# Attention and a routed expert layer on one core: gate data in the rows, gated copies, gathers that add

## The reference, cut to what matters

```python
    x = x + _L0_xcond_ref(_layernorm(x, axis=-1), ctx_2048, ctx_2048, itok_B_779_1933)
    x = x + _L0_ffn_ref(_layernorm(x, axis=-1), L0_ffn_gate_w, L0_ffn_w1, L0_ffn_w2, L0_ffn_w3)

    # attention
    s = SCALE * jnp.log(k_length.astype(jnp.float32))[:, None, None, None]
    attn = jax.nn.softmax(s * jnp.einsum('bhdq,bhdk->bhqk', qh, kh), axis=-1)
    out = jnp.einsum('bhqk,bhdk->bhdq', attn, vh)
    # experts
    probs = jax.nn.softmax(jnp.einsum('ti,ei->te', xt, gate_w), axis=-1)
    expert_weights, expert_indices = jax.lax.top_k(probs, 2)
    expert_weights = expert_weights / expert_weights.sum(axis=-1, keepdims=True)
    y[e] = (silu(xt @ w1[e].T) * (xt @ w3[e].T)) @ w2[e].T
    out = sum over the two chosen experts of expert_weights * y[expert]
```

## Time and profile before

| what | value |
|---|---|
| median of 3 runs | 1231.14 us (1230.88 to 1231.62) |
| the profiled execution | 1232.27 us, of which the span from first to last instruction is 1230.7 us |
| mean granted TensorE clock | 0.951 |
| busy, of the span | TensorE 1035.8 us (84%), VectorE 810.9 (66%), GpSimd 638.4 (52%), ScalarE 410.7 (33%) |

### The profile page before, as it was taken

How to read it: one execution, slowest core, us unless ns; L and a number is a source line. 1 busy time by engine, 2 the same in 40 slices (tenths; PEclk the granted TensorE clock), 3 DMA queues, 4 the chain that set the end, 5 groups by cost and what they waited for, 6 DMA issues and landing times.

```text
span 1230.7 us, 19877 instructions
## 1 busy us (share of the span) xinstructions
PE 1035.8 (84%) x5081; PEld 413.9 (34%) x5082; DVE 810.9 (66%) x953; ACT 410.7 (33%) x734; POOL 638.4 (52%) x578
## 2 busy tenths in 40 slices
PE   1799988999998998832999999999999999999910
PEld 0123322333333333211444444444444444444400
DVE  5877877888888887213853954938677395953354
ACT  3266666666666676721111111111100111011100
POOL 6454766676767762322841834807566182830055
PEclk9699999999999999975999999999999999999965
DMA  6465655565555552105875756647666575753387
GB/s 175 153 223 150 186 153 175 174 189 181 175 177 181 179 150 70 48 27 161 203 141 143 185 132 171 171 96 212 153 197 176 147 191 149 191 133 86 71 227 257
DMA packets 212839, 195.58 MB, mean 159 GB/s; under 512 B 137376, under 2 KB 176288, under 8 KB 207392
## 3 DMA queue, kind: packets, MB, share of 16 engines
q1 hardware_dynamic: 198624, 123.80, 38.5%
q0 software_dynamic: 14176, 71.31, 17.7%
HBM read 111.44 MB, written 52.95 MB: 134 GB/s over the span
## 4 chain that ended last, share of the span: by engine, by line
PE 49%; POOL 20%; DMA 11%; issue 10%; DVE 7%; POOLq 2%; ACT 1%; SPq 1%; DVEq 0%
PE rows L1072 23%; PE heads_out L1072 12%; POOL W L423 7%; PE heads_out L989 4%; PE scores L976 4%; DVE nm L717 3%; PE rows L962 3%; DMA rb<-recips_dram 3%; POOL W L422 3%; DMA recips_dram<-rden 2%; DMA U<-wpack_dram 2%; POOL us L500 1%; POOL us L497 1%; PE misc L1039 1%; POOL U L422 1%
## 5 line engine op out<-in xcount | busy, mean ns | idle before, releaser
L1072 PE MATMUL rows<-W,U 128*128 (+1 forms) x1776 | 391.9, 381 | 23.6 <-DMA U<-stage 19.5
L717 DVE TENSOR_REDUCE nm<-rows 128x2 f32<-128x1024 f32 x256 | 304.2, 1216 | 61.2 <-PE rows L962 53.1
L598 ACT ACTIVATE W<-scores 128x512 f32<-128x512 f32 x512 | 283.9, 596 | 153.0 <-PE scores L976 151.7
L1072 PEld LDWEIGHTS rows<-W,U 128*128 128x128 bf16 x1776 | 174.3, 98 | 236.0 <-issue 30.4
L663 ACT ACTIVATE U<-rows 128x512 f32<-128x512 f32 x78 | 46.4, 597 | 520.3 <-PE rows L1072 511.5
L962 PE MATMUL rows<-W,U 96*128 96x512 bf16 x512 | 151.6, 400 | 71.0 <-DVE nm L717 43.6
L1072 PE MATMUL heads_out<-W,U 128*128 x888 | 199.4, 381 | 13.3 <-issue 10.6
L423 POOL TENSOR_TENSOR W<-U,W 128x2048 bf16<-128x2048 f32 x42 | 172.6, 4110 | 7.7 <-POOL W L422 7.7
L900 DVE TENSOR_TENSOR U<-rows,U 128x512 f32<-128x512 f32 x78 | 53.6, 687 | 183.6 <-ACT U L663 183.5
L976 PE MATMUL scores<-U,W 128*128 128x512 bf16 x512 | 168.1, 386 | 5.6 <-ACT W L598 4.7
L907 DVE TENSOR_TENSOR U<-U 128x512 bf16<-128x512 f32 x78 | 162.7, 2086 | 2.7
(11 more groups left out here) (146 smaller groups left out, 676.4 us busy)
## 6 DMA issues: line engine op xcount, KB each, us to landing
U<-wpack_dram POOLq DMA_DIRECT2D x42, 1024.0 KB, 5.8
parts_dram<-U SPq DMA_DIRECT2D x32, 384.0 KB, 3.9
U<-parts_dram SPq DMA_DIRECT2D x32, 384.0 KB, 3.9
W<-parts_dram SPq DMA_DIRECT2D x32, 384.0 KB, 5.0
stage<-slots_dram SPq DMA_DIRECT2D x39, 256.0 KB, 2.8
expert_out_dram<-U SPq DMA_DIRECT2D x39, 256.0 KB
parts_dram<-U SPq DMA_DIRECT2D x32, 256.0 KB, 4.0
stage<-wpack_dram POOLq DMA_DIRECT2D x12, 512.0 KB, 4.8
```

The source lines that it names most:

```text
L598: s.activation(probs[:, w % 2, j, kk, :], sc[u % 2][:, :], ACT.Exp) \
L717: v.tensor_reduce(nm[:, bb.parity, 2 * k:2 * k + 2], p1[k % 2][:, :].rearrange("p (c k) -> p c k", c=2), AX_X, ALU.max, negate=True).then_ ...
L1072: ins = m.matmul(bank, part_of(s_part, k), W[:, bass.ds(at_w, 512)], start=(k == 0 and n == 0), stop=(k == n_chunks - 1 and n == 2))
```

## The change

Five things are changed.

Rows of z get two more columns (`ROW` = D + 2): the exponential of the second score minus the first, and the first expert's number. VectorE takes the difference where it copied the scores, ScalarE the exponential, GpSimd copies the number, once a batch before the scatters. In the expert stage `row_gates` computes for each tile the gate of each of its rows, in four steps on one column, and `take_y` multiplies by it. An SP row load waits until that tile's predecessor in the buffer has been read.

`stores_needed` computes, between tiles 1 and 2, how many tiles must be stored before each batch can be gathered. Gathers are then issued batch by batch with `compute_op=ALU.add` straight into x in SBUF; the second gather of a batch waits for its first. VectorE's final passes go, and SP stores a batch when its second gather has landed.

The queries of batch 0 are split by VectorE; GpSimd's constants come before the rest of its work of that slot; the number tables come earlier on VectorE, and ScalarE does the zero rows.

Every second zero fill goes to ScalarE's queue.

Tile 0 is turned before the fills are waited for, and its low part comes before the last step of the tables.

```diff
+    ROW = D + 2
-    zs = nc.dram_tensor("slots_dram", [E * REG, D], F32, kind="Internal").ap()
+    zs = nc.dram_tensor("slots_dram", [E * REG, ROW], F32, kind="Internal").ap()
...
-            def load_row(t, par):
+            def load_row(t, par, later=True):
+                if later:
+                    sp.wait_ge(S["row_read"], t - 1)
+                    sp.nop().then_inc(S["sp_held"], 1)
...
             sp.dma_start(xrow[:, 0, :], zs[0:P, :]).then_inc(xrow_in[0], 16)
-            sp.wait_ge(S["zero_out"], 16 * (1 + T - SURE + E))
+            turn_x(0, 0, first=True)
+            sp.wait_ge(S["zero_out"], 16 * (1 + T - SURE + E // 2))
+            sp.wait_ge(S["zero_act"], 16 * (E // 2))
             sp.wait_ge(S["tab_ready"], 1)
-            load_row(1, 1)
-            for t in range(2):
-                turn_x(t, t, first=True)
-                load_row(t + 2, t)
+            load_row(1, 1, later=False)
+            load_row(2, 0)
+            turn_x(1, 1, first=True)
+            load_row(3, 1)
...
-            with sp.Fori(0, B) as b:
-                sp.wait_ge(S["comb_done"], b + 1)
+            for b in range(B):
+                sp.wait_ge(second_in[b % 4], b // 4 * 16 + 16)
...
+                    if pbt.within(0, 0):
+                        hold(S["prep_steps"], st.done)
+                        g.nop().then_inc(S["first_scale"], 1)
+                        constants()
+                if pbt.within(1, B - 1):
...
                     hold(S["idx_ready"], b.n - 1)
+                    g.tensor_copy(z[:, b.parity, D + 1:D + 2],
+                                  experts2[:, bass.ds(pv2.n, 1), 0:1].rearrange("p o a -> p (o a)")) \
+                        .then_inc(S["row_steps"], 1)
+                    hold(S["row_steps"], b.n - 1)
+                    hold(S["row_gate"], b.n - 1)
...
+            hold(S["needs_ready"], 1)
+            hold(S["x1_kept"], B)
+            def add(b, a, landed):
+                pool.indirect_dma_start(
+                    out=xres[:, b, :], out_offset=None, in_=ys[:, :],
+                    in_offset=bass.IndirectOffsetOnAxis(ap=fidx[:, b, a:a + 1], axis=0), compute_op=ALU.add) \
+                    .then_inc(landed[b % 4], 16)
+            def add_second(b):
+                hold(first_in[b % 4], b // 4 * 16 + 16)
+                add(b, 1, second_in)
             for b in range(B):
+                for par in range(2):
+                    stored = pool.value_load(btab[0:1, par, b:b + 1], min_val=16, max_val=16 * ((T + 1) // 2))
+                    hold(y_out[par], stored)
                 if b >= 4:
-                    hold(S["comb_done"], b - 3)
-                gather(b, b % 4)
+                    hold(second_in[b % 4], b // 4 * 16)
+                add(b, 0, first_in)
+                if b >= 2:
+                    add_second(b - 2)
+            add_second(B - 2)
+            add_second(B - 1)
...
+                    act.wait_ge(S["consts"], 2)
+                    for rows_ in (W[96:128, half + 16384:half + 24576], U[96:128, 0:4096].bitcast(BF16)):
+                        s.activation(rows_, zero[96:128, 0:1].to_broadcast([32, 8192]), ACT.Copy) \
+                            .then_inc(S["rows_set"], 1)
...
+                if pv2.within(0, B - 1):
+                    act.wait_ge(S["margin_ready"], b.n - 1)
+                    s.activation(z[:, b.parity, D:D + 1], margin[:, b.parity:b.parity + 1], ACT.Exp) \
+                        .then_inc(S["row_gate"], 1)
...
+            act.wait_ge(S["cv_zero"], 1)
+            act.wait_ge(S["zero_ready"], 1)
+            for e in range(1, E, 2):
+                r = act.value_load(etab[0:1, 0, e:e + 1], min_val=0, max_val=E * REG - P)
+                act.dma_start(zs[bass.ds(r, P), :], cv[:, :]).then_inc(S["zero_act"], 16)
...
+                if b.within(-3, -3):
+                    dve.wait_ge(S["first_scale"], 1)
+                    q_steps = Steps(dve.wait_ge, S["first_steps"], 0, 5)
+                    pt = parts[:, 0]
+                    q_steps.step(v.tensor_scalar(us[:, :], xres[:, 0, :], psc[:, 3:4], psc[:, 2:3], ALU.add, ALU.mult))
+                    q_steps.step(v.tensor_copy(pt[:, 0, :], us[:, :]))
+                    q_steps.step(v.tensor_tensor(us[:, :], us[:, :], pt[:, 0, :], ALU.subtract))
+                    q_steps.step(v.tensor_copy(pt[:, 1, :], us[:, :]))
+                    q_steps.step(v.tensor_tensor(pt[:, 2, :], us[:, :], pt[:, 1, :], ALU.subtract))
...
                 if b.within(-2, -2):
-                    set_rows()
+                    v.memset(mask_sum[:, :], 0.0).then_inc(S["rows_set"], 1)
+                    number()
...
+            def row_gates(t, par):
+                other, first = xrow[:, par, D:D + 1], xrow[:, par, D + 1:D + 2]
+                own = gates[:, bass.ds(t, 1)]
+                v.tensor_scalar(own, first, expt[:, bass.ds(t, 1)], other, ALU.is_equal, ALU.max) \
+                    .then_inc(S["gate_steps"], 1)
+                v.tensor_scalar(total[:, :], other, 1.0, None, ALU.add).then_inc(S["row_read"], 1)
+                dve.wait_ge(S["row_read"], t + 1)
+                v.reciprocal(total[:, :], total[:, :]).then_inc(S["gate_steps"], 1)
+                dve.wait_ge(S["gate_steps"], t * 3 + 2)
+                v.tensor_tensor(own, own, total[:, :], ALU.mult).then_inc(S["gate_steps"], 1)
...
-                v.tensor_copy(yb[:, par, :], ob[:, :]).then_inc(S["yb_ready"], 1)
+                v.tensor_scalar(yb[:, par, :], ob[:, :], gates[:, bass.ds(t, 1)], None, ALU.mult).then_inc(S["yb_ready"], 1)
...
                 if x:
                     x_low(t + 2, par)
+                    row_gates(t + 2, par)
...
+            def stores_needed():
+                order = tio[:, 0, 0:B]
+                dve.wait_ge(S["last_counted"], 1)
+                link(v.tensor_tensor(until, order.unsqueeze(2).to_broadcast([P, B, B]),
+                                     order.unsqueeze(1).to_broadcast([P, B, B]), ALU.is_ge))
+                link(v.tensor_tensor(until, until, sc[0][:, 0:B].unsqueeze(1).to_broadcast([P, B, B]), ALU.mult))
+                link(v.tensor_reduce(cum_b, until, AX_X, ALU.add))
+                link(v.tensor_tensor(until, cum_b.unsqueeze(2).to_broadcast([P, B, B]),
+                                     tio[:, 1, 0:B].unsqueeze(1).to_broadcast([P, B, B]), ALU.is_gt))
+                link(v.tensor_reduce(need_b, until, AX_X, ALU.add))
+                link(v.tensor_scalar(need_b, need_b, before_last[:, 0:1], None, ALU.add))
+                link(v.tensor_copy(odd_i, need_b))
+                link(v.tensor_scalar(odd_i, odd_i, 1, None, ALU.bitwise_and))
+                link(v.tensor_copy(odd_b, odd_i))
+                for par, op in enumerate((ALU.add, ALU.subtract)):
+                    link(v.tensor_tensor(parts_b, need_b, odd_b, op))
+                    link(v.tensor_scalar(btab[:, par, :], parts_b, 8.0, None, ALU.mult))
+                v.nop().then_inc(S["needs_ready"], 1)
...
             tile(0, 0, first=True)
             tile(1, 1, early=True)
+            stores_needed()
             tile(2, 0, early=True)
...
+            pe.wait_ge(S["last_ready"], 1)
+            m.matmul(sc[0][:, 0:B], onesb[:, :], last_b[:, :], start=True, stop=True).then_inc(S["last_counted"], 1)
```

133 lines of the change are left out of this document (57 added, 76 removed).

## The result

The changed kernel is slower: 1242.76 us (median of 20 runs, 1231.24 to 1252.85) against 1231.57 us for the kernel before beside it (20 runs), a ratio of 1.0065 with a 95% interval of 1.0042 to 1.0089. Measured again later the ratio was 1.0078 (1.0033 to 1.0123). The forecast was 1201.5 us. The profiled execution took 1245.81 us, with a span of 1244.3.

The account below looks back on a forecast made before the run. Waits bound five stages: GpSimd at the start and in slots, fills, TensorE in expert tiles, then gathers and output. Terms -6.1 + 3.1 - 6.4 - 1.7 + 8.5 + 0 - 27.0 = -29.6 gave 1201.5 us; range 1189 to 1248.

Parts of the forecast that it names:

- The tail, -27.0: After the last expert tiles: gathers issued early, priced as plain ones, would end the kernel at 1203.7 against 1230.7 us.
- rival 2: Tail: accumulation is dear, the last twelve gathers cost twice the price, 1212 us; sign: landings over 8 us; chance 0.15.
- The slots, +3.1: Attention slots: copy and waits before each scatter cost 0.52 us a batch, paid in six periods where GpSimd is the chain.
- Rival 4: Start and attention slots: the slots take the 6 us back because a transfer binds, 1208 us; chance 0.07.
- `stores_needed`, +8.5: Between tiles 1 and 2: eleven small VectorE steps take 15 us beside GpSimd's split; slack leaves +8.5, from +2 to +13.
- The +6.8: Forecast change from tile 0's product to the last expert's first copy of y, the fourth stretch: 8.5 - 1.7 + 0.
- The gates, 0: Expert tiles: four one-column VectorE steps a tile fit idle time and holes beside GpSimd's split; cost 0, to +5.
- The disputed point: Tile gates: whether one-column VectorE scalar operations wait for GpSimd; forecast that they do not, from 154 against 168 ns.
- rival 1: Expert splits: one-column gate steps wait for GpSimd, 7 us more for two tiles of each split, 1262 us; chance 0.20.
- the narrow hole: Gap of 0.2 us between GpSimd's split steps, at 853.12, where the gates' two-input product was to fit after waiting 1.91.
- The transition, -6.4 and -1.7: Attention to experts: tile 0 ahead of the fills starts TensorE 6.4 us earlier; the first down product's wait of 1.7 goes.
- The start, -6.1: Before the first row products: VectorE preparing batch 0's queries saves 2.3 us, moving the number tables 3.8.

## Why the prediction was wrong

**The tail, -27.0: the step that failed.** It reads "I take the plain price, since the two VectorE passes a batch that leave could at best shorten it". The adding gather costs 1.55 us of queue in place of 0.95, and beside tiles it lands in 8.4 us, not 5.1. Both lay in the step's own upper bound (twice the transfer, twice the issue), but that bound came to only +10, and rival 2 charged the price to the last twelve gathers alone (1212 us). It met the last tiles too: +7.4 us to the last copy, and +14.2 from there to the end, 21.6 against the same kernel with plain gathers (12.8 to 22.4 over the nine profiles with early adding gathers). Rival 2 named the mechanism, and its sign, landings over 8 us, came. The rest of the term was near: the routing (37 tiles used, 37 forecast), and -23.2 with plain gathers. Of the 32 gathers, 26 were issued before the outputs began, but only 20 before the last used tile's copy (24 forecast before the last tile). SP did come to the outputs only behind its last tile store, at 1218.40, but in the end the chain runs through the gathers.

**The slots, +3.1: too small, and by another mechanism.** They lost 10.45. The term treated the slots as bound by GpSimd alone and priced the 0.52 us a batch on its chain; it did not look at TensorE's idle gap at the head of a slot, which is 1.99 us and more in six slots of the changed kernel and in two of the kernel before. The clock fell in three of those six and in neither of the two, and those slots were 2 to 5 us longer. Filling the gap gave back 8 us by the ratios, 13 by the medians on one chip. Rival 4 (the slots take the start's gain back because a transfer binds) came nearest, with the chance 0.07: the reciprocals' transfer is in the chain of the long slots, and the filled gap suggests that the fallen clock puts it there. The rows' data has a part in the loss (1245.8 against 1228.2 us side by side), but by which way, beyond its own steps, stays open.

**`stores_needed`, +8.5: the mechanism right, the size too large.** There are thirteen steps, not eleven; they took 13.9 us (15 forecast). Of that 4.9 us reached TensorE. That the whole stretch grew by 8.4 against the kernel with the steps moved is partly luck. The term also took the good end of its own slack (15 - 4.3 - 2 = 8.7).

**A wait in no term.** Tile 1's down product waits 5.13 us and runs 2.7 us longer at the lower clock, 7.8 us in all. This is the largest part of the fourth stretch's +13.0, and the forecast has nothing for it. It had tile 0's second half through VectorE before the split begins, and that came, but tile 2's low part stands right behind it and met the split's first step. The +6.8 came as near as it did because `stores_needed` was overpriced.

**The gates, 0: not refuted, not priced.** The disputed point went as argued: one-column steps of one source took 0.14 to 0.27 us beside GpSimd's steps, without a wait, in all 39 tiles, and rival 1 fell with it. The Trainium skill (VectorE: DVE Perf Modes, What auto-detection actually checks) has a single-source step use both ports if its outermost dimension that is not 1 is even or equal on both sides; a single column has no such dimension, so the page leaves the case open, and the trace settles it for these steps. But the product of two inputs missed the narrow hole that the term gave it and waited up to 3.25 us in the first split; what that costs TensorE no run separates.

**The transition, -6.4 and -1.7.** The gap at the transpose went; scatters 0.7 and their landing 1.5 us later, and some tenths, took half of it back: -2.9. The -1.7 came: the first down product starts 23.3 us behind the first tile product in place of 25.2, without a wait. The weights' loads began 9.7 us behind it (9.8 forecast). Alone, the part gave 5 to 8 us.

**The start, -6.1:** -5.45, by its two terms.

By the measured terms: -5.45 + 10.45 - 2.9 + 13.0 - 1.55 = +13.6. With plain gathers, and the additions left out, the tail came near the forecast and the kernel was faster than before (0.9902); the versions that gather plainly and do add are faster still.

## What to carry to other kernels

An operation that no row of the trace shows should be priced by a kernel that has it alone before a change rests on it; and a price in transfer time must be charged to everything that shares the DMA engines, not only to the operation's own chain. For work that is moved into a free stretch, ask beside which steps of another engine it will wait there: the same thirteen steps cost 13.9 us beside a GpSimd split and 4.0 three tiles later, where GpSimd idles. One profile against another can't price a term of a few us: two kernels with the same code in the tiles differed by 8 us there, all at one wait.
